# Values and gates in one product, and a new order of TensorE's work in the first pass of a macaron block

## The chip, the cores and the metric

One core of one Trainium2 chip. The time is the device time of one launch, in microseconds; the kernel before has a median of 1885.43 us over 3 runs (1883.06 to 1886.68).

## The reference, cut to what matters

The input x is 2 x 1024 tokens of 512 numbers. Three layers follow each other: half an FFN, an attention, and the same half FFN again.

```python
x = x + 0.5 * ffn(layernorm(x)); x = x + attn(layernorm(x)); x = x + 0.5 * ffn(layernorm(x))

def ffn(x):                       # 8 groups, 64 experts, 8 of them taken
    scores = softmax(x @ gate_w.T); top 8 -> w_e
    flat = w_e[:, inv_map]        # [token, group, 8]
    scalar = flat.sum(-1); soft = softmax(where(flat == 0, -1e9, flat))
    xg = x + soft @ mask_up_w     # per group
    a = silu(xg @ gate_proj.T) * (xg @ up_proj.T)
    return sum over groups of scalar * (a @ down_proj.T)

def attn(x):                      # gated linear attention, 4 heads, 64 values each
    q, k, v = x @ Wq, x @ Wk, x @ Wv
    gk = log_sigmoid(x @ Wgk1 @ Wgk2 + bgk2) / 16
    o = chunkwise recurrence over chunks of 64 tokens, with decay exp(gk)
    o = rms_norm(o) * Wnorm * silu(x @ Wg)
    return o @ Wo
```

All matrix products keep float32 accuracy: each operand is split into a high and a low part, and three products (high by high, high by low, low by high) are added in PSUM. `three` issues them.

## The kernel before, in words

The 2048 tokens are 4 blocks of 512. A **pass** (`p` or `q`, 0 to 7, called the first pass, pass 2 and so on in the text) is one FFN over one block; four of the passes (q = 1, 2, 4, 5) also carry the attention of a block. A pass has 22 **chunks** (`c`; `n` counts them over all passes) of 128 hidden rows of the FFN. For chunk n TensorE runs, in this order: `main` into bank GB (the gate sum, 12 matmuls of 512 columns), `soft` into the same bank (one matmul, line 1244: the routed part, whose weights are the product of mask_up_w and the chunk's weights), `main` into UB (the up sum, 12), `soft` into UB, and `down(n-1)` (12, into the four banks YB). Behind each of the three is a **slot**: `pieces(3n)`, `pieces(3n+1)`, `pieces(3n+2)` run the step k = 3c, 3c+1, 3c+2 of the attention of this pass and of the router of the next one. Step k does its part on each engine at that engine's place in its own program. Each engine works strictly in program order.

For chunk n ScalarE computes `sig` = Silu of GB, VectorE computes `act_t` = UB x sig x s_bc (`gate`), ScalarE rounds it into `a_hi` (`round_a`), VectorE subtracts into `a_lo` (`rest_a`), and `down` reads both.

In the first pass the weights are not yet split. Per chunk c SyncE's queue loads raw gate/up weights (`raw_gu`, a part of b_all) and down weights (`raw_d`, a part of k_all); ScalarE writes the high part (`gu_hi`, `d_hi`), VectorE the low part (`gu_lo`, `d_lo`), in `wt` or `tw`, and `dt`. Then TensorE multiplies mask_up_w by the chunk's weights (`masked`, 8 matmuls of 256 columns, lines 1229 and 1230), VectorE masks the result (`m_mask`, gt from bank and q_all), ScalarE and VectorE split it (`m_top`, `m_rest`, wt from gt), and `soft` reads it. GpSimd's queue stores the split weights to `scr_w` and `scr_d`, from where the later passes load them (`load_w`, `load_d`). Order in the first pass: TensorE ends chunk c with `masked(c+1)`; ScalarE has `gu_hi(c+1)` behind the Silu of chunk c; VectorE begins chunk c with `gu_lo(c+1)`, then `gate(c)`.

Router of the next pass, steps: 28 statistics, 31 norm, 32, 33, 35, 36 the four transposes with high and low parts of x (x_hi, x_lo), 38 logits, 39 to 50 the routing. Attention, steps: 7 to 11 transposes, 13 and 15 values, 14 the low-rank decay input, 16 to 19 the four decay logits, 20 and 21 gates, 22 to 29 queries and keys, from 30 on the recurrence. Its weights come in seven slabs per block, loaded by GpSimd's queue (`load_t`) and split at the steps that `SPLIT` names.

All engines are ordered by semaphores that only count up. TensorE's waits that matter here: `masked(c+1)` waits for `gu_lo(c+1)`; `soft` in the first pass waits for `m_rest` of its chunk (m_ok); the transposes of the router wait for the norm (xn_ok) and for the low part of the tile before.

Of the kernel before, what the change touches and what calls it, by code (L numbers as in the profile page):

```python
# [14 lines left out]
P = 128  # L15
# [26 lines left out]
S_V, S_G, S_QK, S_WO = 0, 1, 2, 6  # L42
# [20 lines left out]
def build(nc, x, wgu, wdn, wat, w_gate, w_mup, w_gk1, w_gk2, bgk, wnorm, inv, c_id, c_mask, c_reset, c_iota, out):  # L63
    with ExitStack() as ctx:
# [94 lines left out]
        def first_w(c):  # L159
# [34 lines left out]
        v_mm, g_mm, vt_ok, gt_ok, gtw_ok, z1_ok, zs_hi_ok, zs_ok, z_mm, zmin_ok, zabs_ok, zexp_ok, zln_ok = (  # L194
            sem(n) for n in ("v_mm", "g_mm", "vt_ok", "gt_ok", "gtw_ok", "z1_ok", "zs_hi_ok", "zs_ok", "z_mm", "zmin_ok",
# [44 lines left out]
        SPLIT = {4: S_V, 9: S_G, 16: S_QK, 22: S_QK + 1, 24: S_QK + 2, 26: S_QK + 3, 28: S_WO}  # L240
# [4 lines left out]
        def _(sp):  # L245
            def raw(c):
                j, half = c // 2, c % 2
                wait(sp, gu_lo_ok, c - 1)
                sp.dma_start(raw_gu[:, half, :], wgu[half, j]).then_inc(raw_gu_in[half], 16)
                wait(sp, d_lo_ok, c - 1)  # L250
                sp.dma_start(raw_d[:, half, :], wdn[half, j]).then_inc(raw_d_in[half], 16)
# [19 lines left out]
            raw(0)  # L271
            sp.dma_start(mask.rearrange("p a b -> p (a b)"), c_mask).then_inc(ld_mask, 16)
            raw(1)
            for c in range(2, CH):
                raw(c)
                if c == 2:
                    sp.dma_start(xr(1), x_t[1]).then_inc(ld_x[1], 16)
                if c == 4:
                    sp.dma_start(xr(2), x_t[2]).then_inc(ld_x[2], 16)
# [21 lines left out]
        def _(pool):  # L301
# [26 lines left out]
            def attention(t, q):  # L328
# [5 lines left out]
                load_t(t, S_V)  # L334
                rstd_of(LN_T[t])
                for n in range(S_G, S_QK + 2):
                    load_t(t, n)
                pool.wait_ge(gt_ok, 2 * t + 2)
# [44 lines left out]
            for q in range(1, PHASES):  # L383
                if FINAL[q - 1]:
                    store_out(q - 1)
# [8 lines left out]
        def _(act):  # L394
# [17 lines left out]
            def t_hi(t, s):  # L412
# [5 lines left out]
                elif s == S_QK + 1:  # L418
                    act.wait_ge(g_mm, 2 * t + 2)
                elif s == S_QK:  # L420
                    act.wait_ge(v_mm, 2 * t + 2)
# [4 lines left out]
                elif s == S_V:  # L426
# [63 lines left out]
            def attention(t, k, q):  # L490
                r, s = LN_T[t], (q + 1) % 2
                if k in SPLIT:
                    t_hi(t, SPLIT[k])
                if k in (7, 8, 10, 11):
# [4 lines left out]
                elif k == 14:  # L499
# [15 lines left out]
                elif k in (20, 21):  # L515
                    i = k - 20
                    act.wait_ge(g_mm, 2 * t + i + 1)
                    if i == 0:
                        wait(act, og_ok, t * H)
                    nc.scalar.activation(gt[:, 2 * i:2 * i + 2, :].rearrange("p a b -> p (a b)"), (W1, W0)[i][:],  # L520
                                         ACT.Silu).then_inc(gt_ok, 1)
# [111 lines left out]
            for p in range(PHASES):  # L633
                for c in range(CH):
# [6 lines left out]
                    round_a(n)  # L641
                    if n + 2 < PHASES * CH:
# [6 lines left out]
                    if p == 0 and 0 < c < CH - 1:  # L649
# [3 lines left out]
        def _(dve):  # L653
# [172 lines left out]
            def attention(t, k, q):  # L826
# [17 lines left out]
                elif k in (13, 15):  # L844
                    i = (k - 13) // 2
                    dve.wait_ge(v_mm, 2 * t + i + 1)
# [3 lines left out]
                    v = W0[:].rearrange("p (a v) -> p a v", v=DV)  # L850
                    z = vtz[:, 2 * i:2 * i + 2, :, :, :].rearrange("p t h r v -> p (t h) r v")
                    nc.vector.tensor_copy(z[0:CK, :, 0, :], v[0:CK, :, :])
                    nc.vector.tensor_copy(z[CK:P, :, 1, :], v[CK:P, :, :]).then_inc(vt_ok, 1)
                elif k == 14:
# [132 lines left out]
            for p in range(PHASES):  # L987
                for c in range(CH):
# [3 lines left out]
                    gate(n)  # L992
                    pieces(3 * n + 1)
                    rest_a(n)
                    if n == 1:
# [4 lines left out]
                    if p == 0 and 0 < c < CH - 1:  # L1000
# [6 lines left out]
        def _(pe):  # L1007
# [71 lines left out]
            def attention(t, k, q):  # L1079
                r, s = LN_T[t], (q + 1) % 2  # L1080

                def slab(n):
# [282 lines left out]
```

## Time and profile before

| | |
|---|---|
| median of 3 runs | 1885.43 us |
| profiled execution, its own time | 1883.3 us |
| span of its trace | 1881.6 us |
| TensorE busy | 1856.3 us (99%), 8896 matmuls |
| VectorE, ScalarE, GpSimd busy | 802.2, 528.2, 140.0 us |
| moved by DMA | 390.68 MB, mean 208 GB/s |
| mean granted TensorE clock | 0.997 |

A matmul's duration in the trace is that of the whole pipeline (390 ns for 512 columns), so neighbours overlap; how fast they follow each other is read from the difference of their starts. A line shows start and duration in us, engine, line, operation, output and inputs by name, partitions by elements, how many, and in brackets how long the engine was idle before it and what it waited for. PE is TensorE, ACT is ScalarE, DVE is VectorE, POOL is GpSimd, SP is SyncE; SPq is SyncE's DMA queue.

### The profile page before, as it was taken

The numbers are of one execution on the slowest core, as the hardware profiler recorded it, in microseconds if no ns is written. First come the engines' busy times: TensorE is split into PE (matmuls) and PEld (weight loads), VectorE is DVE, ScalarE is ACT, GpSimd is POOL, SyncE is SP. The second block draws the span as 40 slices with busy tenths as digits, with TensorE's granted clock in tenths as the row PEclk, the third lists the DMA queues.
The fourth block names the chain that finished last, engine by engine and source line by source line (L and its number), as shares of the span: only waits on it lengthen the run. The fifth ranks groups of instructions, "written<-read, shape, count | busy, mean of one in ns | idle before, by whom it ended". The sixth has DMA issues, their size and how long they took to land.

```text
span 1881.6 us, 22831 instructions
## 1 busy us (share of the span) xinstructions
PE 1856.3 (99%) x8896; PEld 1552.5 (83%) x8896; DVE 802.2 (43%) x1478; ACT 528.2 (28%) x802; POOL 140.0 (7%) x246
## 2 busy tenths in 40 slices
PE   6999999999999999999999999999999999999999
PEld 5887888888888888888888888888888888888887
DVE  6455553545354543323334455354544323322222
ACT  3333423433124432112212533123432111311111
POOL 1131110100000000000010000000000000000000
PEclk9999999999999999999999999999999999999999
DMA  6987875445564455576676454564455566567665
GB/s 198 318 279 247 276 283 199 154 156 179 191 232 151 159 172 193 193 248 210 210 254 222 164 193 163 188 231 168 156 173 179 200 239 214 210 214 261 220 235 175
DMA packets 94187, 390.68 MB, mean 208 GB/s; under 512 B 11936, under 2 KB 12320, under 8 KB 71552
## 3 DMA queue, kind: packets, MB, share of 16 engines
q1 hardware_dynamic: 54096, 286.74, 43.1%
q10 hardware_dynamic: 27600, 47.15, 9.6%
q0 software_dynamic: 12384, 55.32, 7.8%
q8 instruction: 72, 1.18, 0.3%
q14 instruction: 35, 0.29, 0.0%
HBM read 347.36 MB, written 41.81 MB: 207 GB/s over the span
## 4 chain that ended last, share of the span: by engine, by line
PE 94%; DVE 3%; DMA 1%; ACT 1%; issue 1%; SPq 0%; ACTq 0%; DVEq 0%
PE bank L1012 27%; PE bank L1014 27%; PE bank L1013 27%; PE bank L1244 4%; PE bank L1022 1%; PE bank L1185 1%; PE bank L1177 1%; PE bank L1184 1%; DMA b_all<-wgu 1%; PE bank L1171 1%; DVE act_t L655 0%; PE bank L1042 0%; PE bank L1229 0%; PE bank L1043 0%; PE bank L1230 0%
## 5 line engine op out<-in xcount | busy, mean ns | idle before, releaser
L1012 PE MATMUL bank<-x_hi,wt 128*128 128x512 f32 x1328 | 525.2, 395 | 0.2 <-issue 0.2
L1014 PE MATMUL bank<-x_lo,wt 128*128 128x512 f32 x1328 | 518.5, 390 | 0.0
L1013 PE MATMUL bank<-x_hi,wt 128*128 128x512 f32 x1328 | 518.2, 390 | 0.0
L655 DVE TENSOR_TENSOR act_t<-bank,sig 128x512 f32<-128x512 f32 x176 | 121.6, 691 | 557.9 <-PE bank L1244 556.3
L1014 PEld LDWEIGHTS bank<-x_lo,wt 128*128 128x128 f32 x1328 | 249.5, 188 | 53.0
L1012 PEld LDWEIGHTS bank<-x_hi,wt 128*128 128x128 f32 x1328 | 249.8, 188 | 49.9 <-issue 0.6
L1013 PEld LDWEIGHTS bank<-x_hi,wt 128*128 128x128 f32 x1328 | 249.9, 188 | 49.1
L1012 PE MATMUL bank<-dt,a_hi 128*128 128x512 f32 x704 | 279.7, 397 | 0.3 <-DVE a_lo L655 0.3
L1014 PE MATMUL bank<-dt,a_hi 128*128 128x512 f32 x704 | 275.4, 391 | 0.0
L1013 PE MATMUL bank<-dt,a_lo 128*128 128x512 f32 x704 | 274.6, 390 | 0.0
L581 ACT ACTIVATE sig<-bank 128x512 f32<-128x512 f32 x176 | 105.3, 598 | 479.4 <-PE bank L1244 479.4
L396 ACT ACTIVATE a_hi<-act_t 128x512 fp32r<-128x512 f32 x176 | 110.9, 630 | 372.5 <-DVE act_t L655 370.6
L655 DVE TENSOR_TENSOR a_lo<-act_t,a_hi 128x512 fp32r<-128x512 f32 x176 | 121.4, 690 | 157.9 <-ACT a_hi L396 157.3
L1014 PEld LDWEIGHTS bank<-dt,a_hi 128*128 128x128 f32 x704 | 132.2, 188 | 28.2
L1012 PEld LDWEIGHTS bank<-dt,a_hi 128*128 128x128 f32 x704 | 132.6, 188 | 26.5 <-issue 0.7
L1013 PEld LDWEIGHTS bank<-dt,a_lo 128*128 128x128 f32 x704 | 132.6, 188 | 25.9
L1244 PE MATMUL bank<-softT,wt 128*128 128x512 f32 x352 | 138.5, 395 | 9.6 <-DVE wt L655 9.3
L655 DVE TENSOR_TENSOR act_t<-s_bc,act_t 128x512 f32<-128x512 f32 x176 | 121.8, 692 | 6.3 <-DMA s_bc<-scr_s 0.3
L1244 PEld LDWEIGHTS bank<-softT,wt 128*128 128x128 f32 x352 | 66.2, 188 | 25.7 <-DVE wt L655 11.6
L1012 PE MATMUL bank<-x_hi,tw 128*128 128x512 f32 x208 | 82.2, 395 | 0.0
L1013 PE MATMUL bank<-x_hi,tw 128*128 128x512 f32 x208 | 82.1, 395 | 0.0
L1014 PE MATMUL bank<-x_lo,tw 128*128 128x512 f32 x208 | 82.0, 394 | 0.0
(178 smaller groups left out, 1748.5 us busy)
## 6 DMA issues: line engine op xcount, KB each, us to landing
wt<-scr_w SPq DMA_DIRECT2D x154, 1152.0 KB, 5.2
dt<-scr_d SPq DMA_DIRECT2D x154, 512.0 KB, 5.2
s_bc<-scr_s ACTq DMA_DIRECT2D x128, 256.0 KB, 5.3
state<-wat POOLq DMA_DIRECT2D x28, 512.0 KB, 5.3
scr_w<-wt POOLq DMA_DIRECT2D x12, 1024.0 KB, 5.1
b_all<-wgu SPq DMA_DIRECT2D x22, 512.0 KB, 7.4
scr_d<-dt POOLq DMA_DIRECT2D x22, 512.0 KB, 7.1
scr_w<-tw POOLq DMA_DIRECT2D x10, 1024.0 KB, 4.7
```

The costliest lines, as they stand in the source:

```text
L396: return nc.scalar.activation(dst, src, ACT.Copy)
L581: nc.scalar.activation(sig[:], g_bank(n)[:], ACT.Silu).then_inc(sig_ok, 1)
L655: return nc.vector.tensor_tensor(dst, a, b, op)
L1012: mm(dst, wh, xh, start=start, stop=False)
L1013: mm(dst, wl, xh, start=False, stop=False)
L1014: return mm(dst, wh, xl, start=False, stop=stop)
L1022: ins = nc.tensor.transpose(b[:, cols(k)], xn[:, i % 2, cols(k)], ident[:])
L1171: ins = mm(W0[:, cols(i)], b_all[:, h, cols(i)], q_all[:, h, cols(i)], start=True, stop=True)
L1177: ins = mm(W0[:, cols(i)], k2t[:, i, :], vtz[:, i, h, :, :], start=True, stop=True)
L1184: mm(W0[:, cols(i)], scm[:, h % 2, i, :], vtz[:, i, h, :, :], start=True, stop=False)
L1185: ins = mm(W0[:, cols(i)], q_all[:, h, cols(i)], state[:, h % 2, 2 * i:2 * i + 2, :], start=False, stop=True)
L1244: return mm(b[:], m[:, c0:c0 + P], softT[:, p % 2, c % 2, :], start=False, stop=True)
```

## The change

- The weights of values and gates are laid side by side: one product of 512 columns gives both for 128 tokens. It runs in steps 13 to 16, four groups of 12 matmuls into bank W0. VectorE copies the values out, then ScalarE takes Silu of the gates; the next group waits for that. Steps 20 and 21 fall away. Each of the two slabs holds two of the four parts of the inner dimension, so both are needed from step 13 on; the query/key slabs are split in steps 18 and 20 rather than 16 and 22.
- The first slab of an attention is loaded before the output stores of the pass before.
- First pass: SyncE issues gate/up load c+1 before down load c, and the inputs of blocks 1 and 2 behind chunks 4 and 7 rather than 2 and 4.
- First pass: `m_mask`, `m_top` and `m_rest` of chunk 2 stand in chunk 0's part of the program rather than in chunk 1's.
- First pass: TensorE runs both sums, with step 3n between them, and only then both soft matmuls. The other passes keep their order.

```diff
@@ -39,7 +39,7 @@
 SLABS = 7
-S_V, S_G, S_QK, S_WO = 0, 1, 2, 6
+S_VG, S_QK, S_WO = 0, 2, 6
@@ -237,16 +237,19 @@
-        SPLIT = {4: S_V, 9: S_G, 16: S_QK, 22: S_QK + 1, 24: S_QK + 2, 26: S_QK + 3, 28: S_WO}
+        SPLIT = {4: S_VG, 9: S_VG + 1, 18: S_QK, 20: S_QK + 1, 24: S_QK + 2, 26: S_QK + 3, 28: S_WO}
...
         def _(sp):
-            def raw(c):
+            def raw_gate_up(c):
                 j, half = c // 2, c % 2
...
                 sp.dma_start(raw_gu[:, half, :], wgu[half, j]).then_inc(raw_gu_in[half], 16)
+
+            def raw_down(c):
+                j, half = c // 2, c % 2
                 wait(sp, d_lo_ok, c - 1)
@@ -268,15 +271,20 @@
                 sp.dma_start(xr(0)[:, i, :], x_t[0][:, i, :]).then_inc(ld_x0[i], 16)
-            raw(0)
+            raw_gate_up(0)
+            raw_down(0)
             sp.dma_start(mask.rearrange("p a b -> p (a b)"), c_mask).then_inc(ld_mask, 16)
-            raw(1)
+            raw_gate_up(1)
+            raw_down(1)
+            raw_gate_up(2)
             for c in range(2, CH):
-                raw(c)
-                if c == 2:
-                    sp.dma_start(xr(1), x_t[1]).then_inc(ld_x[1], 16)
-                if c == 4:
-                    sp.dma_start(xr(2), x_t[2]).then_inc(ld_x[2], 16)
+
+                if c + 1 < CH:
+                    raw_gate_up(c + 1)
+                raw_down(c)
+                if c in (4, 7):
+                    b = (4, 7).index(c) + 1
+                    sp.dma_start(xr(b), x_t[b]).then_inc(ld_x[b], 16)
             for p in range(1, PHASES):
@@ -325,17 +333,19 @@
-            def attention(t, q):
+            def first_slab(t):
...
                     pool.wait_ge(o_ok, t * H)
-                load_t(t, S_V)
+                load_t(t, S_VG)
+
+            def attention(t, q):
                 rstd_of(LN_T[t])
-                for n in range(S_G, S_QK + 2):
+                for n in range(S_VG + 1, S_QK + 2):
                     load_t(t, n)
-                pool.wait_ge(gt_ok, 2 * t + 2)
+                pool.wait_ge(gt_ok, (t + 1) * NT)
                 if t == 0:
@@ -381,6 +391,8 @@
             for q in range(1, PHASES):
+                if q in ATT:
+                    first_slab(ATT[q])
                 if FINAL[q - 1]:
@@ -415,15 +427,13 @@
                     act.wait_ge(k_mm, t * H + s - S_QK - 1)
-                elif s == S_QK + 1:
-                    act.wait_ge(g_mm, 2 * t + 2)
-                elif s == S_QK:
-                    act.wait_ge(v_mm, 2 * t + 2)
+                elif s >= S_QK:
+                    act.wait_ge(vg_mm, (t + 1) * NT)
                 elif t == 0:
...
                     act.wait_ge(st_w[2 + s], 16 * len(range(2 + s, CH, 4)))
-                elif s == S_V:
+                elif s == S_VG:
                     act.wait_ge(k_mm, t * H)
@@ -491,12 +501,18 @@
                     t_hi(t, SPLIT[k])
+                if k in (13, 14, 15, 16):
+                    i = k - 13
+                    act.wait_ge(vt_ok, t * NT + i + 1)
+                    if i == 0:
+                        wait(act, og_ok, t * H)
+                    nc.scalar.activation(gt[:, i, :], W0[:, 2 * P:4 * P], ACT.Silu).then_inc(gt_ok, 1)
                 if k in (7, 8, 10, 11):
...
                     hi(r, i, s, (W0, W1)[i % 2])
-                elif k == 14:
+                if k == 14:
                     act.wait_ge(z1_ok, t + 1)
@@ -512,13 +528,6 @@
                         nc.scalar.activation(spl[:], spl[:], ACT.Ln, bias=1.0).then_inc(zln_ok, 1)
-                elif k in (20, 21):
-                    i = k - 20
-                    act.wait_ge(g_mm, 2 * t + i + 1)
-                    if i == 0:
-                        wait(act, og_ok, t * H)
-                    nc.scalar.activation(gt[:, 2 * i:2 * i + 2, :].rearrange("p a b -> p (a b)"), (W1, W0)[i][:],
-                                         ACT.Silu).then_inc(gt_ok, 1)
                 elif 22 <= k <= 29:
@@ -639,6 +648,8 @@
                     round_a(n)
+                    if n == 0:
+                        m_top(2)
                     if n + 2 < PHASES * CH:
@@ -646,7 +657,7 @@
                     pieces(3 * n + 2)
-                    if p == 0 and 0 < c < CH - 1:
+                    if p == 0 and 1 < c < CH - 1:
                         m_top(c + 1)
@@ -841,17 +852,16 @@
                         norm(r, i + 2, xb)
-                elif k in (13, 15):
-                    i = (k - 13) // 2
-                    dve.wait_ge(v_mm, 2 * t + i + 1)
+                if k in (13, 14, 15, 16):
+                    i = k - 13
+                    dve.wait_ge(vg_mm, t * NT + i + 1)
                     wait(dve, o_ok, t * H)
...
                         dve.wait_ge(zero_ok, 3)
-                    v = W0[:].rearrange("p (a v) -> p a v", v=DV)
-                    z = vtz[:, 2 * i:2 * i + 2, :, :, :].rearrange("p t h r v -> p (t h) r v")
-                    nc.vector.tensor_copy(z[0:CK, :, 0, :], v[0:CK, :, :])
-                    nc.vector.tensor_copy(z[CK:P, :, 1, :], v[CK:P, :, :]).then_inc(vt_ok, 1)
-                elif k == 14:
+                    v = W0[:, 0:2 * P].rearrange("p (h v) -> p h v", v=DV)
+                    nc.vector.tensor_copy(vtz[0:CK, i, :, 0, :], v[0:CK, :, :])
+                    nc.vector.tensor_copy(vtz[CK:P, i, :, 1, :], v[CK:P, :, :]).then_inc(vt_ok, 1)
+                if k == 14:
                     dve.wait_ge(zs_hi_ok, t + 1)
@@ -990,14 +1000,18 @@
                     gate(n)
+                    if n == 0:
+                        m_mask(2)
                     pieces(3 * n + 1)
                     rest_a(n)
+                    if n == 0:
+                        m_rest(2)
                     if n == 1:
...
                     pieces(3 * n + 2)
-                    if p == 0 and 0 < c < CH - 1:
+                    if p == 0 and 1 < c < CH - 1:
                         m_mask(c + 1)
@@ -1079,10 +1093,11 @@
-                def slab(n):
-                    n += t * SLABS
+                def slab(s):
+
+                    n = t * SLABS + s
                     pe.wait_ge(t_lo_ok, n + 1)
-                    w = tw[:, n % 2, :].rearrange("p (a k c) -> p a k c", a=2, k=KC)
+                    w = tw[:, n % 2, :].rearrange("p (a k c) -> p a k c", a=2, k=2 if s < S_QK else KC)
                     return w[:, 0, :, :], w[:, 1, :, :]
@@ -1099,20 +1114,18 @@
                     turn(r, i, (W0, W1)[i % 2])
-                elif k in (13, 15):
-                    n = (k - 13) // 2
-                    if n == 0:
+                if k in (13, 14, 15, 16):
+                    i = k - 13
+                    if i == 0:
                         pe.wait_ge(x_lo_ok, r * NT + 3)
...
                         pe.wait_ge(x_lo_ok, r * NT + 4)
-                        pe.wait_ge(vt_ok, 2 * t + 1)
-                    hi, lo = slab(S_V)
-                    for j in range(2):
-                        for kk in range(KC):
-                            ins = three(W0[:, cols(j, 2 * P)], xk(s, kk, cols(2 * n + j)), (hi[:, kk, :], lo[:, kk, :]),
-                                        kk == 0, kk == KC - 1)
-                    ins.then_inc(v_mm, 1)
-                elif k == 14:
+                        pe.wait_ge(gt_ok, t * NT + i)
+                    for kk in range(KC):
+                        hi, lo = slab(S_VG + kk // 2)
+                        ins = three(W0[:], xk(s, kk, cols(i)), (hi[:, kk % 2, :], lo[:, kk % 2, :]), kk == 0, kk == KC - 1)
+                    ins.then_inc(vg_mm, 1)
+                if k == 14:
                     pe.wait_ge(x_lo_ok, r * NT + 4)
@@ -1125,24 +1138,15 @@
                     elif h == 1:
-                        pe.wait_ge(vt_ok, 2 * t + 2)
+                        pe.wait_ge(gt_ok, (t + 1) * NT)
                     else:
...
                     mm((W1, W0)[h % 2][:], gk2_s[:, cols(h)], zs[:], start=True, stop=True).then_inc(z_mm, 1)
-                elif k in (20, 21):
-                    n = k - 20
-                    pe.wait_ge(zabs_ok, t * H + 3 + n)
-                    hi, lo = slab(S_G)
-                    for j in range(2):
-                        for kk in range(KC):
-                            ins = three((W1, W0)[n][:, cols(j, 2 * P)], xk(s, kk, cols(2 * n + j)), (hi[:, kk, :], lo[:, kk, :]),
-                                        kk == 0, kk == KC - 1)
-                    ins.then_inc(g_mm, 1)
                 elif 22 <= k <= 29:
...
                     if h == 0:
-                        pe.wait_ge(gt_ok, 2 * t + 1 + is_k)
+                        pe.wait_ge(zabs_ok, t * H + 3 + is_k)
                     else:
@@ -1172,7 +1176,7 @@
                         pe.wait_ge(sc_cp, t * H + h + 1)
-                        pe.wait_ge(vt_ok, 2 * t + 2)
+                        pe.wait_ge(vt_ok, (t + 1) * NT)
                         for i in range(NT):
@@ -1296,11 +1300,15 @@
                         main(GB, 0, p, c)
-                    soft(g_bank(n), 0, p, c).then_inc(g_ok, 1)
+                    if p:
+                        soft(g_bank(n), 0, p, c).then_inc(g_ok, 1)
                     pieces(3 * n)
...
                         main(UB, P, p, c)
+                    if p == 0:
+
+                        soft(g_bank(n), 0, p, c).then_inc(g_ok, 1)
                     soft(u_bank(n), P, p, c).then_inc(u_ok, 1)
```

## Rows read from the trace of the kernel before

**Rows 1.** Page, part 1: busy time of each engine, share of the span, instructions.

```profile
PE 1856.3 (99%) x8896; PEld 1552.5 (83%) x8896; DVE 802.2 (43%) x1478; ACT 528.2 (28%) x802; POOL 140.0 (7%) x246
```

**Rows 2.** Waits of TensorE: total us, times, longest.

```profile
PE bank L1022 <- DVE o_all L708: 10.3, 7, 6.5
PE bank L1244 <- DVE wt L655: 9.3, 5, 6.1
```

**Rows 3.** TensorE by stretch: stretch, length, busy (matmuls), granted clock, DMA.

```profile
40.30:46.40 6.10, 0.01 (x1) 0.66 0.91 257
46.40:52.50 6.10, 6.10 (x14) 0.50 0.96 375
```

**Rows 4.** Stretch behind the first pass: PE, PEld, DVE, ACT, POOL, clock, DMA.

```profile
254.00:1881.00 1627.00, 1622.13 (x7782) 1358.91 (x7780) 664.46 (x1220) 437.29 (x658) 93.60 (x157) 1.00 0.58 199
```

**Rows 5.** Timeline of TensorE, pass 2, first group of values and what follows.

```profile
295.61 0.28 PE L1012 MATMUL bank<-tw,x_hi 128*128 128x256 f32 x1
295.72 0.28 PE L1013 MATMUL bank<-tw,x_lo 128*128 128x256 f32 x1
...
298.48 0.40 PE L1012 MATMUL bank<-dt,a_hi 128*128 128x512 f32 x1
298.71 0.40 PE L1013 MATMUL bank<-dt,a_lo 128*128 128x512 f32 x1
```

**Rows 6.** Timeline of VectorE, a copy of 256 columns out of PSUM.

```profile
28.09 0.42 DVE L756 COPY tb<-bank 128x256 f32<-128x256 f32 x1 [0.61 <-PE bank L1059]
```

**Rows 7.** Timeline, pass 2, last decay logit and the chunk's a_lo.

```profile
321.37 0.39 PE L1131 MATMUL bank<-zs,gk_s 128*128 128x512 f32 x1
...
331.50 0.69 DVE L655 TENSOR_TENSOR a_lo<-act_t,a_hi 128x512 fp32r<-128x512 f32 x1 [7.85 <-ACT a_hi L396]
```

**Rows 8.** Timeline of the start: TensorE, VectorE, ScalarE, SyncE's queue.

```profile
37.41 0.40 PE L1012 MATMUL bank<-x_hi,tw 128*128 128x512 f32 x1
...
41.37 0.51 SPq L249 DMA_DIRECT2D b_all<-wgu  x1
...
45.02 0.42 DVE L655 TENSOR_TENSOR gt<-bank,q_all 128x256 f32<-128x256 f32 x1
...
46.38 0.80 PE L1244 MATMUL bank<-softT,wt 128*128 128x512 f32 x1 [6.09 <-DVE wt L655]
...
54.33 1.06 ACT L396 ACTIVATE tw<-b_all 128x1024 fp32r<-128x1024 f32 x1 [6.52 <-DMA b_all<-wgu]
...
65.84 0.39 PE L1244 MATMUL bank<-softT,wt 128*128 128x512 f32 x1
```

**Rows 9.** Timeline, chunk 7 of the first pass: soft, gu_lo, masked.

```profile
101.38 0.39 PE L1244 MATMUL bank<-softT,wt 128*128 128x512 f32 x1
...
103.38 1.23 DVE L655 TENSOR_TENSOR wt<-b_all,wt 128x1024 fp32r<-128x1024 f32 x1 [3.22 <-ACT wt L396]
...
107.27 0.29 PE L1229 MATMUL bank<-wt,og 128*128 128x256 f32 x1
```

**Rows 10.** Timeline, chunks 10 and 11: soft, norm (x2), soft, gu_lo.

```profile
131.23 0.50 PE L1244 MATMUL bank<-softT,wt 128*128 128x512 f32 x1 [0.71 <-DVE wt L655]
...
136.07 1.00 DVE L708 TENSOR_SCALAR o_all<-x_res,mv,rstd 128x512 f32<-128x512 f32 x2
...
141.39 0.40 PE L1244 MATMUL bank<-softT,wt 128*128 128x512 f32 x1
...
144.95 1.22 DVE L655 TENSOR_TENSOR wt<-b_all,wt 128x1024 fp32r<-128x1024 f32 x1
```

**Rows 11.** Timeline, end of the first pass: soft, mask store, first load, first matmul.

```profile
237.29 0.39 PE L1244 MATMUL bank<-softT,wt 128*128 128x512 f32 x1
...
241.34 0.54 POOL L316 DMA_DIRECT2D scr_w<-wt  x1
...
247.65 3.00 SPq L260 DMA_DIRECT2D wt<-scr_w  x2
...
253.18 0.47 PE L1012 MATMUL bank<-x_hi,wt 128*128 128x512 f32 x1 [0.22 <-issue]
```

**Rows 12.** Timeline of TensorE, chunk 14 of the first pass.

```profile
175.99 0.50 PE L1244 MATMUL bank<-softT,wt 128*128 128x512 f32 x1 [1.38 <-DVE wt L655]
```

More of the change, by code:

```diff
@@ L193, in build @@
         dve_step = sem("dve_step")
-        v_mm, g_mm, vt_ok, gt_ok, gtw_ok, z1_ok, zs_hi_ok, zs_ok, z_mm, zmin_ok, zabs_ok, zexp_ok, zln_ok = (
-            sem(n) for n in ("v_mm", "g_mm", "vt_ok", "gt_ok", "gtw_ok", "z1_ok", "zs_hi_ok", "zs_ok", "z_mm", "zmin_ok",
+        vg_mm, vt_ok, gt_ok, gtw_ok, z1_ok, zs_hi_ok, zs_ok, z_mm, zmin_ok, zabs_ok, zexp_ok, zln_ok = (
+            sem(n) for n in ("vg_mm", "vt_ok", "gt_ok", "gtw_ok", "z1_ok", "zs_hi_ok", "zs_ok", "z_mm", "zmin_ok",
                              "zabs_ok", "zexp_ok", "zln_ok"))
@@ L1335 @@
     heads = [np.concatenate([fold(f[n][:, h * P:(h + 1) * P]) for n in ("attn_Wq", "attn_Wk")], axis=-1) for h in range(H)]
-    wat = np.stack([w.reshape(P, GW) for w in (fold(f["attn_Wv"]), fold(f["attn_Wg"]), *heads, fold(f["attn_Wo"]))])
+    values_gates = np.concatenate([fold(f["attn_Wv"]), fold(f["attn_Wg"])], axis=-1)
+    wat = np.stack([w.reshape(P, GW) for w in (values_gates[:, 0:2], values_gates[:, 2:4], *heads, fold(f["attn_Wo"]))])
     inv = f["ffn_inv_map"]
```

## Prediction

> **What bounds the kernel now.** I read the page's first part, then the waits of TensorE, the granted clock by stretch, and the timeline of the first pass. TensorE is busy in 1856.3 of 1881.6 us, VectorE in 43%, ScalarE in 28% [rows 1]. So only two things can shorten the run: fewer TensorE cycles, or less TensorE waiting. Its waits [rows 2] come to about 22 us: 10.3 before transposes, 6.5 of them for the first input, and 9.3 before the routed (soft) matmuls, L1244, one of them 6.1 us. A stretch view shows a second price of that one: in the 6.1 us after it the clock is 0.50, which is 1.2 GHz [rows 3]. From 254 us to the end TensorE is busy in 1622 of 1627 us [rows 4]: there is nothing to win there but cycles. Spacings below are differences of starts: 120 ns for 256 columns (24 matmuls from 295.61 to 298.48), 227 ns for 512 (26 from 101.38 to 107.27) [rows 5, 9].
>
> **Part 1: values and gates joined.** Before, each attention block runs 96 matmuls of 256 columns, in four groups of 24; after, 48 of 512, in four groups of 12. One group of 24 takes 298.48 - 295.61 = 2.87 us [rows 5]; twelve of 512 take 12 x 0.227 = 2.72. That is 0.15 x 4 groups x 4 blocks = **-2.4 us**. Bounds: -3 and 0; it is nothing if the joined ones come at 0.239.
> At this place the Trainium skill can be weighed (page "TensorE: Matmul & The Clock Gate", section "Back-to-back issue gap"): a warm matmul takes N / 2.4 + 2.5 ns. By it 24 take 2.62 us and 12 wide ones 2.59, so the join would give 0.5 us over all blocks. The rows are slower than the rule at both widths, and more so at 256.
>
> Does a wait take its place? The four groups share one bank: group i+1 waits for ScalarE's gate of group i, which waits for VectorE's two value copies, and ScalarE's a_hi and VectorE's a_lo of the chunk are queued behind them. Nearest row: 0.42 us for 256 columns out of PSUM [rows 6]. So 0.2 drain + 0.43 + 0.43 + 0.45 = 1.5 us, under the 12 matmuls (2.72 us) between two groups. Hidden with 1.2 us to spare; without that cover each of 12 gaps would pay the difference. a_lo is late by 3 us and needed 10 later.
> The gates' 5.8 us also leave the place between the fourth decay logit and the first query, where ScalarE does Abs, Exp and Ln and only then a_hi. There the last logit matmul starts at 321.37 and a_lo is ready at 332.19: 10.8 us [rows 7]; a slab's splitting, now queued in front, adds 0.3. The down product that needs it now comes after 51 matmuls, 11.6 us. Hidden by 0.5 us. Taken: 0, bounds 0 and +4 us. The first slab's load goes ahead of four output stores on GpSimd's queue, once; no TensorE wait hangs on either: 0.
>
> **Part 2: start of the first pass.** The 6.1 us wait is for VectorE's m_rest of chunk 2, whose m_mask ran at 45.02 [rows 8]. It stands in the program behind gate(1), a_lo, the decay weights and d_lo. TensorE had done its masked product by 37.4. The change issues m_mask after gate(0), at 38.3; m_top follows a_hi(0) on ScalarE, m_rest ends at 40.2. That delays d_lo(0) and what is behind it by some 0.9 us. Meanwhile TensorE has 24 matmuls ahead of the soft pair, from 37.41 to 42.86. So this wait goes, and the low clock with it. Next late would be gate/up load 3: issued at 41.37, because SyncE's queue stood behind a down load that waits for d_lo(0), and used at 54.33 as it landed [rows 8]. The change issues it at about 17.8, when gu_lo(1) is done. The two input loads of 1 MB go later, to chunks 4 and 7; the first is needed in chunk 9. From 42.86: soft pair 0.45, down(0), down(1) 5.45, masked 0.97, gate and up sums 5.45, soft of chunk 3 at 55.2, its second at 55.4. Before, that second one started at 65.84. **-10.4 us**.
>
> **Part 3: the steady first pass, where the new order costs.** T is the start of a chunk's gate soft matmul. It releases Silu, then gu_hi, then gu_lo, which ends at T + 3.23 [rows 9]. The next chunk's masked product (L1229) needs gu_lo, and the sums wait behind it. Before, 26 matmuls lay between, and it came at T + 5.9 [rows 9]. Now 14 do: T + 3.18. It waits until 3.29, and a first pair after a wait is some 0.09 slower: 0.19 us. In chunks 3 to 8 this is +0.9 (0.2 of waiting there is in the old time), in 17 to 20 +0.8: **+1.7 us**. In chunks 9 and 13 to 15 VectorE's chain bounds as before and starts 0.2 us sooner: **-0.6 us**.
> In chunk 10 the first router transpose stands behind down. It needs VectorE's norm, behind gate(10), done at 136.6 = T + 5.4 [rows 10]. Before, TensorE came at T + 5.9. Now it comes at T + 3.2 and waits until T + 5.2: +2.0. In chunk 11 gu_lo ends at 146.17 = T + 4.78, because x_lo before it waits for ScalarE [rows 10]; the masked product, one transpose (0.44) later than T + 3.2, waits 1.1. Another transpose that needs x_lo loses 0.3. With the slower first pairs: **+3.7 us**.
>
> **Part 4: the end of the first pass.** The first weight load of pass 2 is issued at 247.65, when the store of mask part 20 has landed; that store was issued at 241.34 behind the 1 MB store that follows gu_lo(21). TensorE starts on it at 253.18, 0.4 us late [rows 11]. From the soft matmul of chunk 20 (237.29) that chain is 15.89 us. TensorE will need 3.29 + 0.09 + 0.97 + 5.45 + 0.45 + 2.72 = 13.0 us from there, not 15.5. The wait becomes 2.9: **+2.5 us**. The chain itself isn't changed.
>
> **Sum.** -10.4 + 1.7 - 0.6 + 3.7 + 2.5 = -3.1 in the first pass, -2.4 in the joined products: -5.5 us. Two new holes, of 2.0 and 2.9 us, may cost clock. After the hole of 6.1 us 13 matmuls ran at 0.427 instead of 0.227, 2.6 us [rows 3]; a hole of 1.4 us cost none [rows 12]. Bounds 0 and 5.2; I take 1.3, half of one, since the 2.9 lies between them. Result -4.2: profiled execution 1883.3 - 4.2 = 1879.1 us (its span is 1.7 less). The median shown, 1885.43, lies 2.1 above that execution: **1881.2 us**.
>
> **Rivals.**
> A: the late costs don't come (parts 3 and 4 near 0): -10.4 - 2.4 = -12.8, 1872.6 us; with half of them 1876. For it: VectorE is idle over half the time. Against: the order of gu_lo, norm and the last stores stays, and their times are rows. 0.25.
> B, slower: the cover behind the decay logits. It decides from 0.5 us of slack. If ScalarE's Abs, Exp, Ln chain comes 2.5 us later than reckoned, TensorE stands 2 us before down in each of four blocks: +8, the sum +3.8, 1889 us. For it: it is the thinnest cover of the passes with attention, and slab splitting is queued before it. Against: 0.3 of shift is all that I find. 0.1.
> C: both new holes bring the low clock in full: -5.5 + 5.2 = -0.3, 1885.1, no change. For it: 2.0 and 2.9 are longer than any later hole of the trace. 0.2.
> D: the join gives nothing, the wide matmuls coming at 0.239: -5.5 + 2.4 + 1.3 = -1.8, 1883.6. Against: 512 columns out of tw run at 0.227 elsewhere. 0.05. The Trainium skill's rule of part 1 would give 1883.1; the rows contradict it.
> My own sum: 0.4.
>
> **Chances.** 0.2% is 3.8 us, about what a measurement of this kernel can tell from none. Faster (under 1881.7): A's 0.25 and somewhat more than half of mine, with a remainder, 0.54. Within: 0.34. Slower: B and a little, 0.12. Range 1875.0 to 1886.0: beyond half of A at the low end, C at the high one.
>
> **What would show it.** Right: no wait near 40 us and full clock there; the soft pair of chunk 3 at 55; masked products waiting 0.1 us each for VectorE's wt or tw; a transpose wait of 2 us in chunk 10; a wait of 2.5 to 3 us at the first load of pass 2; joined matmuls 0.227 apart and no wait before down in the attention passes. Wrong: a wait still at chunk 2's soft matmuls, down products waiting for a_lo in passes 2, 3, 5 and 6, or a long stretch at 1.2 GHz after a short hole.

## The result, and the profile after

The changed kernel takes **1887.84 us** (median of 22 runs, 1885.17 to 1890.78), the kernel before, on the same chip, 1885.13 (22 runs, 1882.40 to 1888.55). The ratio is 1.0015, 95% interval 1.0009 to 1.0021: 2.7 us slower, within the 3.8 us called no change, and 6.6 us above the forecast of 1881.2. The profiled execution took 1887.89 us, its span 1886.2.

The first part of the page of the changed kernel, the answer to [rows 1]:

```profile
PE 1857.4 (98%) x8704; PEld 1540.2 (82%) x8704; DVE 810.2 (43%) x1494; ACT 529.6 (28%) x810; POOL 140.6 (7%) x246
```

There are 192 matmuls fewer (48 x 4 blocks), and yet TensorE is busy 1.1 us longer. Its waits, the answer to [rows 2] (total us, times, longest):

```profile
PE bank L1036 <- DVE o_all L719: 12.1, 7, 6.5
PE bank L1026 <- DVE a_lo L666: 5.0, 5, 1.2
PE bank L1026 <- issue: 3.4, 1, 3.4
PE bank L1248 <- DVE wt L666: 1.9, 3, 1.0
PE bank L1056 <- DVE x_lo L666: 1.5, 1, 1.5
PE bank L1233 <- DVE wt L666: 0.9, 1, 0.9
```

The 6.1 us before a soft matmul are gone. In their place stand 5.0 us before `down` for a_lo, which was 0.3 before, 3.4 us at one load, and 1.8 us more before a transpose.

Where the time came and went is read best from the start of the same matmul in both traces (the later of the two soft matmuls of chunk n, which both kernels run in the same place). After minus before, us:

| chunk | 3 | 9 | 10 | 11 | 12 | 17 | 21 | 22 | 30 | 52 | 110 | 175 |
|---|---|---|---|---|---|---|---|---|---|---|---|---|
| before at | 65.84 | 123.70 | 134.31 | 144.83 | 155.35 | 211.42 | 249.85 | 258.97 | 352.61 | 611.88 | 1234.23 | 1871.81 |
| after - before | -9.81 | -8.86 | -9.12 | -7.00 | -5.44 | -5.07 | -4.30 | +1.73 | +2.46 | +3.19 | +3.87 | +4.59 |

So 9.8 us are won by chunk 3. Of these 5.5 are lost over the rest of the first pass, 6.0 more at its end, between chunks 21 and 22, and 0.72 in each of the four attention blocks.

**The start** (timeline of the changed kernel; the answer to [rows 8]):

```profile
39.04 0.42 DVE L666 TENSOR_TENSOR gt<-bank,q_all 128x256 f32<-128x256 f32 x1
...
43.25 0.62 PE L1248 MATMUL bank<-softT,wt 128*128 128x512 f32 x2
...
45.48 1.05 ACT L408 ACTIVATE tw<-b_all 128x1024 fp32r<-128x1024 f32 x1
46.56 1.23 DVE L666 TENSOR_TENSOR tw<-b_all,tw 128x1024 fp32r<-128x1024 f32 x1
```

The mask product runs at 39.04 instead of 45.02. The two soft matmuls follow behind both sums with no wait in front of them, and the high part of gate/up chunk 3 is written at 45.48, where it stood at 54.33 waiting for its load.

**Chunks 10 and 11** (timeline; the answer to [rows 10]; the bracket is the idle time before the instruction and what ended it):

```profile
125.19 0.40 PE L1248 MATMUL bank<-softT,wt 128*128 128x512 f32 x1
...
129.44 1.21 DVE L719 TENSOR_SCALAR o_all<-x_res,mv,rstd 128x512 f32<-128x512 f32 x2
...
130.23 0.63 PE L1036 MATMUL bank<-ident,o_all 128*128 128x128 f32 x4 [1.91 <-DVE o_all L719]
...
141.16 1.22 DVE L666 TENSOR_TENSOR wt<-b_all,wt 128x1024 fp32r<-128x1024 f32 x1
...
142.43 0.39 PE L1233 MATMUL bank<-wt,og 128*128 128x256 f32 x1 [0.93 <-DVE wt L666]
```

The transpose comes at the end of `down`, 3.2 us behind the soft matmuls, and stands until VectorE's norm is there.

**The end of the first pass** (timeline; the answer to [rows 11]):

```profile
235.53 0.61 PE L1248 MATMUL bank<-softT,wt 128*128 128x512 f32 x2
...
239.58 0.55 POOL L324 DMA_DIRECT2D scr_w<-wt  x1
...
245.11 2.38 SPq L263 DMA_DIRECT2D wt<-scr_w  x2
...
252.11 0.77 PE L1026 MATMUL bank<-x_hi,wt 128*128 128x512 f32 x1 [3.45 <-issue]
```

Behind it, by stretch (stretch, length, PE, PEld, DVE, ACT, POOL, granted clock, DMA share, GB/s):

```profile
252.20:258.00 5.80, 5.80 (x14) 4.54 (x15) 0.00 (x0) 0.00 (x0) 0.00 (x0) 0.50 1.00 361
```

TensorE stood 3.45 us, and then ran at 0.50, which is 1.2 GHz, until 257.8: 13 matmuls at 0.427 instead of 0.227, 2.6 us. The kernel before paid the same 2.6 us behind its 6.1 us wait [rows 3], so nothing is saved there. Experiment 4, where neither stretch exists, is busy for 1854.2 us. Where the rest of the 1.1 us comes from stays open.

**An attention block** (timeline, pass 2; last decay logit, then what a_lo waits for; the answer to [rows 7]):

```profile
319.80 0.39 ACT L509 ACTIVATE gt<-bank 128x256 f32<-128x256 f32 x1 [5.29 <-DVE vtz L863]
...
326.72 1.23 DVE L666 TENSOR_TENSOR tw<-state,tw 128x1024 fp32r<-128x1024 f32 x1 [3.42 <-ACT tw L408]
...
328.18 0.39 PE L1144 MATMUL bank<-zs,gk_s 128*128 128x512 f32 x1
328.25 0.53 POOL L334 DMA_DIRECT2D state<-wat  x1 [39.61 <-DVE tw L666]
...
328.79 2.41 POOL L351 TENSOR_TENSOR gt<-gt,wn 128x1024 f32<-128x1024 f32 x1
329.24 2.51 DVE L666 TENSOR_TENSOR act_t<-s_bc,act_t 128x512 f32<-128x512 f32 x1
...
331.68 0.74 DVE L874 TENSOR_SCALAR tb<-bank,bias 128x512 f32<-128x512 f32 x1
332.51 0.69 ACT L525 ACTIVATE b_all<-bank,bias 128x512 f32<-128x512 f32 x1 [3.12 <-DVE tb L874]
333.22 1.28 ACT L528 ACT_TABLE_LOAD   x1
334.51 1.92 ACT L528 ACTIVATE b_all<-b_all 128x2048 f32<-128x2048 f32 x1
...
340.28 0.69 DVE L666 TENSOR_TENSOR a_lo<-act_t,a_hi 128x512 fp32r<-128x512 f32 x1 [7.86 <-ACT a_hi L408]
341.11 0.47 PE L1026 MATMUL bank<-dt,a_hi 128*128 128x512 f32 x1 [1.16 <-DVE a_lo L666]
```

VectorE's product `act_t<-s_bc,act_t` takes 2.51 us. The same instruction takes 0.69 elsewhere: of the 176 in the launch only the four that meet GpSimd's multiply by Wnorm, one per block, are long. GpSimd's multiply had begun 0.45 us earlier and ended at 331.20. Behind the product wait, one after the other, the last decay logit's copy, Abs, Exp, Ln, a_hi, a_lo and `down`. In the kernel before, the same multiply ran from 334.37 to 336.77, since it waited for the second group of gates (timeline of the kernel before):

```profile
334.37 2.40 POOL L341 TENSOR_TENSOR gt<-gt,wn 128x1024 f32<-128x1024 f32 x1 [18.90 <-ACT gt L520]
```

No product of VectorE with two inputs in SBUF started beside it there. The join makes the last gate ready before the decay logits, at 320.2, and so the gates no longer hold the multiply back. What then sets its moment stands ahead of it in GpSimd's program: the load of the next query/key slab, which waits until VectorE has split the slab before it. That split now stands in step 18 rather than 16. It ends at 327.95, the load is issued at 328.25, and the multiply follows at 328.79, right before the product. In the kernel before this load was issued at 314.94, long before the gates. The order is the same in all four blocks.

### The profile page after: what moved, and what is told of

Read it like the earlier page. It is cut to its first block, busy times and chain, and to the rows that moved or that the text cites. A ratio compares the mean times of both kernels' runs of the same rounds, so it can differ in the third digit from the quotient of the medians.

```text
span 1886.2 us, 22478 instructions
## 1 busy us (share of the span) xinstructions
PE 1857.4 (98%) x8704; PEld 1540.2 (82%) x8704; DVE 810.2 (43%) x1494; ACT 529.6 (28%) x810; POOL 140.6 (7%) x246
## 4 chain that ended last, share of the span: by engine, by line
PE 91%; DVE 4%; ACT 3%; issue 2%; DMA 0%; POOL 0%; ACTq 0%; SPq 0%; DVEq 0%; POOLq 0%
PE bank L1026 26%; PE bank L1028 26%; PE bank L1027 26%; PE bank L1248 4%; PE bank L1036 1%; DVE act_t L666 1%; PE bank L1189 1%; PE bank L1181 1%; PE bank L1188 1%; PE bank L1233 1%; PE bank L1175 1%; PE bank L1234 0%; PE bank L1056 0%; PE bank L1057 0%; ACT b_all L528 0%
## 5 line engine op out<-in xcount | busy, mean ns | idle before, releaser
L1248 PE MATMUL bank<-softT,wt 128*128 128x512 f32 x352 | 134.5, 393 | 2.2 <-DVE wt L666 1.9
L666 DVE TENSOR_TENSOR act_t<-s_bc,act_t 128x512 f32<-128x512 f32 x176 | 129.1, 734 | 6.7 <-DMA s_bc<-scr_s 0.7
```

Source lines behind the costliest of these rows:

```text
L666: return nc.vector.tensor_tensor(dst, a, b, op)
L1248: return mm(b[:], m[:, c0:c0 + P], softT[:, p % 2, c % 2, :], start=False, stop=True)
```

## The experiments

Ten kernels were run, in three groups, each group beside runs of the kernel before on one chip (medians there 1884.86, 1883.97 and 1884.30). A trace's table means the comparison above, against the trace of before.

**1. Without GpSimd's multiply.** This kernel leaves the factor Wnorm out of the attention's output.

```diff
-                pool.wait_ge(gt_ok, (t + 1) * NT)
-                nc.gpsimd.tensor_tensor(gt[...], gt[...], wn[...], ALU.mult).then_inc(gtw_ok, 1)
...
-                dve.wait_ge(gtw_ok, t + 1)
+                dve.wait_ge(gt_ok, (t + 1) * NT)
```

> The changed kernel without GpSimd's multiply of the gates by Wnorm (left out, so the output lacks that factor). Theory L (the port): VectorE's second gate product stood 2.5 us instead of 0.69 because GpSimd's multiply ran at the same time, and that alone makes a_lo late for the down product; then that product takes 0.69 again in all four attention passes, the four waits of 1.2 us before down are gone, and the time is 5.3 us under the changed kernel's 1887.8, so 1882.5. Theory G (the queue: moved gates' Silu and the slab splitting in front of the decay logits make the chain late by themselves): the four waits stay at 1 us or more, and the time is within 1 us of 1887.8.

Measured: 1881.40 us, ratio 0.9979 (0.9970 to 0.9988), 6.8 us under the changed kernel by the ratios. The waits for a_lo are gone, all but the 0.3 us of before, and all 176 products take 0.69. So the multiply is what delays the chain.

**2. The multiply later.** It is issued behind the router's statistics on GpSimd (with the last slab loads ahead of it), where VectorE's gate products are not beside it. Nothing is left out.

```diff
-                [multiply of gt by wn, in attention(t, q)]
+            def norm_weight(t): [the same multiply]
...
                 if q in ATT:
+                    norm_weight(ATT[q])
                     attention_tail(ATT[q])
```

> The changed kernel with the same multiply, but put behind the router's rstd on GpSimd, where VectorE is idle in the trace (about 380 to 385 us in pass 2). Theory L: as without the multiply, 1882.5, no wait before down. A weaker form of it, in which any GpSimd work lengthens the chain, would leave part of the waits or put new ones at the transposes of 390 us (0.7 us each). Theory G: no change, 1887.8.

Measured: 1881.24 us, 0.9980 (0.9972 to 0.9989). The multiply runs at 374.59 in pass 2, with no instruction of VectorE beside it. The place of the old collision in its trace (timeline):

```profile
325.86 0.69 DVE L669 TENSOR_TENSOR act_t<-s_bc,act_t 128x512 f32<-128x512 f32 x1
...
329.31 1.92 ACT L531 ACTIVATE b_all<-b_all 128x2048 f32<-128x2048 f32 x1
...
335.07 0.69 DVE L669 TENSOR_TENSOR a_lo<-act_t,a_hi 128x512 fp32r<-128x512 f32 x1 [7.86 <-ACT a_hi L411]
```

The last decay logit starts at 324.79 in this trace and a_lo ends at 335.76: 10.97 us, the 10.8 of [rows 7] and almost nothing more. In the changed kernel it was 340.97 - 328.18 = 12.79; the difference, 1.82, is that of the product (2.51 - 0.69). Each block now gives -0.72 in the table.

**3. The gate's soft matmul ahead of the up sum again**, in the first pass; all else as changed.

```diff
-                    if p:
-                        soft(g_bank(n), 0, p, c).then_inc(g_ok, 1)
+                    soft(g_bank(n), 0, p, c).then_inc(g_ok, 1)
                     pieces(3 * n)
...
-                    if p == 0:
-                        soft(g_bank(n), 0, p, c).then_inc(g_ok, 1)
```

> The changed kernel with the gate's soft matmul back ahead of the up sum in the first pass; all else as changed. Theory S (the new order costs all through the first pass what the early mask of chunk 2 wins): no wait at the masked products, none of 2 us in chunk 10, the hole at the end of the pass back from 3.6 to about 0.4 us and no low clock behind it. Pass 2 then starts some 9 us under before at chunk 3 and still 9 to 10 under it at the end of the pass; time 1887.8 - 11.5 = 1876.3. A small wait of 0.1 to 0.3 us at chunk 2's soft matmul. Rival R (the order is needed for the start): chunk 2 waits 2 us or more and the gain is under 7 us.

Measured: 1877.43 us, 0.9961 (0.9948 to 0.9975), 10.2 us under the changed kernel by the ratios. In the table it stays at -9.6 from chunk 9 to 13 and at -8.97 at chunk 22, where the changed kernel has +1.73. The holes of chunks 10 and 11 and of the end are gone and the clock is 1.000. The mask's product, now needed sooner, costs one wait, in chunk 2 (timeline of TensorE):

```profile
40.68 0.50 PE L1248 MATMUL bank<-softT,wt 128*128 128x512 f32 x1 [0.38 <-DVE wt L666]
```

**4. The mask's store ahead of the 1 MB store**, at chunk 20 of the changed kernel, on GpSimd's queue: the first load of pass 2 waits for that store.

```diff
+                if c == CH - 2:
+                    store_m(c)
                 if c + 1 < CH:
                     store_w(c + 1)
-                store_m(c)
+                if c != CH - 2:
+                    store_m(c)
```

> The changed kernel with one pair of GpSimd's stores swapped in chunk 20: the mask part goes ahead of the 1 MB of weights. Theory E (the first load of pass 2 waits for the mask store behind the 1 MB store): the hole of 3.6 us at about 248 shrinks to under 1.5 us, and the 13 matmuls at the low clock behind it run at full clock: 2 to 3.6 us plus 2.7 us, so 1881.5 to 1883.2. Rival: the load waits for the weight stores themselves, or the load's own 5 us are the end of the chain; hole within 0.5 us of before, time 1887.8.

Measured: 1883.17 us, 0.9992 (0.9983 to 1.0000), 4.3 us under the changed kernel by the ratios. The hole at the first load is gone, and the next load comes late (waits of TensorE):

```profile
PE bank L1029 <- DMA wt<-scr_w: 1.8, 1, 1.8
```

No low clock follows. So the hole at the first load is a matter of the stores' order, as reckoned, and part of it returns one load later: 2.1 us between chunks 22 and 23 in the table.

**5. Experiments 2 and 3 together.**

> The changed kernel with both: the gate's soft matmul back ahead of the up sum, and the multiply by Wnorm late on GpSimd. If the two costs are separate they add: 1885 - 9.0 (start, measured in the run with the old soft order) - 2.4 (join) = 1873.6, no wait before down, no low clock. If the late multiply meets other VectorE work once the first pass is shorter: 1875 to 1877 with new waits at the transposes of the attention passes.

Measured: 1871.89 us, 0.9934 (0.9920 to 0.9947), 12.4 us faster than before and 1.7 under the forecast sum. The two costs are separate: no wait for a_lo is left but the 0.3 us of before, and the clock is 1.00. Its longest waits of TensorE, and its stretch behind the first pass:

```profile
PE bank L1039 <- DVE o_all L722: 10.0, 7, 6.6
PE bank L1251 <- DVE wt L669: 3.7, 5, 1.4
PE bank L1059 <- DVE x_lo L669: 1.5, 1, 1.5
```

```profile
254.00:1869.00 1615.00, 1611.75 (x7557) 1341.68 (x7556) 665.81 (x1234) 438.47 (x665) 92.79 (x155) 1.00 0.58 198
```

**6. The join and the early first slab alone**: the first pass's order, its loads and its mask as before.

> The join and the first slab alone, on the kernel before (first pass as before). Sum of my reading: -2.4 for the joined products, +5.3 for four waits before down behind GpSimd's multiply: +2.9, 1887.9, with the 6.1 us wait and its low clock as in the kernel before. If the wait before down came only because the passes start at another phase of the transfers, it is gone here: 1882.6.

Measured: 1886.01 us, 1.0012 (1.0003 to 1.0020): the join by itself, with its collision, makes the kernel some 2 us slower. The waits for a_lo are there with the first pass untouched, and so is the old one before soft (waits of TensorE):

```profile
PE bank L1234 <- DVE wt L656: 10.3, 6, 6.5
...
PE bank L1012 <- DVE a_lo L656: 5.0, 5, 1.2
```

In its table each of the four blocks adds 0.70 to 0.72, as in the changed kernel.

**7. The early mask alone**, on the kernel before.

```diff
                     gate(n)
+                    if n == 0:
+                        m_mask(2)
...
-                    if p == 0 and 0 < c < CH - 1:
+                    if p == 0 and 1 < c < CH - 1:
                         m_mask(c + 1)
```

(`m_top` and `m_rest` likewise.)

> The early m_mask, m_top and m_rest of chunk 2 alone, on the kernel before (old order of loads, of soft matmuls, old values and gates). Theory N (the next wait takes its place): gate/up load 3 is still issued at about 41.5 and lands near 54, so the masked product of chunk 3 waits for gu_lo(3) from 49 to 56.6, some 7.5 us, with low clock behind it: the gain is at most 1.2 us, time 1884 to 1885.5. Theory M (the mask alone is the fault): the 6.1 us and the clock are won, 8.7 us, 1876.3.

Measured: 1885.42 us, 1.0004 (0.9995 to 1.0013), no gain (timeline):

```profile
43.32 0.39 PE L1250 MATMUL bank<-softT,wt 128*128 128x512 f32 x1
...
54.25 1.06 ACT L396 ACTIVATE tw<-b_all 128x1024 fp32r<-128x1024 f32 x1 [9.52 <-DMA b_all<-wgu]
55.34 1.23 DVE L657 TENSOR_TENSOR tw<-b_all,tw 128x1024 fp32r<-128x1024 f32 x1 [9.73 <-ACT tw L396]
56.62 0.58 PE L1235 MATMUL bank<-tw,og 128*128 128x256 f32 x1 [7.48 <-DVE tw L657]
```

The wait of 6.1 us before chunk 2's soft matmul has become one of 7.5 us before chunk 3's masked product, because the load of gate/up 3 still lands at 54.

**8. The new order of the loads alone**, on the kernel before (the hunk of SyncE's queue in the diff).

> The kernel before with the new order of the input loads alone; chunk 2's mask stays late. Theory N (the mask's place and the load's place each hide the other's wait, so that only both together give the 10 us; the early mask alone gave nothing): the wait before chunk 2's soft matmul stays, since VectorE's mask product still runs behind gate(1), and gate/up load 3 is no longer late but nobody waited for it. No change, -1 to +0.5 us. Theory M (the loads were the larger half all along, and the early mask is not needed): -8 to -10 us, and no wait near 46 us.

Measured: 1884.15 us, 0.9997 (0.9987 to 1.0007), no gain either: the load is there in time (the high part of gate/up 3 is written at 47.88), and the old wait stays (timeline of TensorE):

```profile
46.55 0.79 PE L1252 MATMUL bank<-softT,wt 128*128 128x512 f32 x1 [6.22 <-DVE wt L663]
```

**9. Both, on the kernel before**, without the join and with the old order of the soft matmuls.

> The early mask of chunk 2 and the new order of SyncE's loads together, on the kernel before, without the new order of the soft matmuls and without the join. Theory N: together they win what neither does alone: soft matmul of chunk 3 some 9.5 us earlier, and 9 us at the end of the pass, 1876.0; chunk 2 waits 0.5 us or less. If the order of the soft matmuls were needed too, chunk 2 would wait over 2 us and the gain would be under 7.

Measured: 1874.75 us, 0.9954 (0.9941 to 0.9967): 8.7 us faster. Two edits that are each worth nothing are worth nearly 9 together.

**10. Experiment 5 with both soft matmuls behind the sums in chunk 2 alone.**

```diff
+                    if n != 2:
                         soft(g_bank(n), 0, p, c).then_inc(g_ok, 1)
                     pieces(3 * n)
...
+                    if n == 2:
+                        soft(g_bank(n), 0, p, c).then_inc(g_ok, 1)
```

> The best version so far (old order of the gate's soft matmuls, GpSimd's multiply late) with the new order of the soft matmuls kept in chunk 2 alone, where the profile of the old order has a wait of 0.5 us for the mask. If the new order helps wherever VectorE's split weights come after the gate sum and hurts only where it shortens the cover of the next chunk: the 0.5 us go, chunk 3's masked product has two matmuls fewer of cover and may wait 0.2 of them; 0 to -0.5 us against that version, so 1871.5. If the order costs in any chunk: +0.2 or more against it, 1872.1 or above. The difference is near what the spans can show; the start of the soft matmul of chunk 3 tells it.

Measured: 1872.06 us, 0.9930 (0.9916 to 0.9945). That can't be told from experiment 5's 0.9934. In the traces the wait before chunk 2's soft matmul is gone, and from chunk 1's second soft matmul to chunk 3's TensorE takes 19.55 us, where experiment 5 takes 20.04. But the same stretch takes 19.89 in experiment 3 and 19.49 in experiment 9, both with the old order: the wait for the mask differs from trace to trace, from 0.55 us to nothing. So whether the new order in chunk 2 is worth 0.5 us or nothing stays open.

## Why the prediction was wrong

Worked out in the prediction's own terms, on the profiled executions, in us (the table of chunks above is called the table):

| term | forecast | measured | read from |
|---|---|---|---|
| start of first pass | -10.4 | -9.8 | table, chunk 3 |
| steady first pass, chunks 3 to 21 | +1.7 - 0.6 + 3.7 = +4.8 | +5.5 | -4.30 + 9.81 |
| end, the hole | +2.5 | +3.2 | from the last matmul's start to the first that uses the load: 3.84, before 0.61 |
| low clock | +1.3 | +2.8 | the rest of 1.73 + 4.30; 13 matmuls x 0.20 are 2.6 of it |
| join, cycles | -2.4 | -2.9 | 4 x (-0.72), experiment 2 |
| join, cover behind the decay logits | 0 | +5.8 | 4 x (0.72 + 0.72), changed kernel and experiment 2 |
| sum (of unrounded terms) | -4.2 | +4.6 | |

**The step that failed** is in part 1: "Hidden by 0.5 us. Taken: 0". The arithmetic of that step was right as far as it went: without the collision the chain takes 10.97 us (experiment 2) where 10.8 and 0.3 were reckoned, and TensorE's 11.6 us cover it. What was left out is where the change moves GpSimd's multiply. It waits for the last gate (`gt_ok` stands in the diff) and stands behind a slab's load. The gates come some 14 us earlier, the load waits for the split that the change puts in step 18, and so the multiply falls on VectorE's product. The chain grows by 1.82 us and eats the 0.5. What is left is 1.32 us of waiting per block, and the first matmuls behind the wait follow each other more slowly, 0.1 more. Experiments 1, 2 and 6 each show that from another side. That the split's step decides the moment is read from the traces; no run has the multiply in its old place in the program and the split elsewhere. Rival B named the right place, the right releaser and the point from which it decides (0.5 us of slack); it had neither this cause nor this size (8 us against 5.8) and was given 0.1. The step's upper bound of 4 us was too low as well.

The row and a rule agree here. VectorE's product was held from 329.24, GpSimd's multiply ended at 331.20, and the product ended 0.55 later. The product just before it, `act_t<-bank,sig`, has one input in PSUM; it also overlapped the multiply and took 0.68, as elsewhere. The Trainium skill, page "SBUF — State Buffer", sections "Who interferes with whom" and "SBUF: two separate sides", states that a VectorE instruction with two SBUF inputs and a GpSimd instruction that reads SBUF exclude each other through a shared port, and that whichever starts second is blocked for the whole of the other. By that rule the question for the join was not only how long the gates take but what VectorE does when the multiply starts.

**The second miss** is the price of a hole: two terms mis-sized, by 0.7 and 1.5 us. The chain behind the hole of 2.9 us was said not to change. From chunk 20's first soft matmul it was 15.89 us and became 252.11 - 235.53 = 16.58. The store of the mask landed sooner (9.58 us from soft to the issue of the load, 10.36 before), but from its issue to TensorE's first matmul the load took 7.00 us, not 5.53. In experiments 1 and 2, whose first pass is the same program, it took 7.28 and 5.92, so its length also differs from trace to trace. DMA engines were busy 0.96 of the time from 247.5 to 252.5, and 0.87 from 248 to 253 before; that this traffic is the cause is argued, not shown. And the low clock came in full, where half was taken. Experiment 2, with a hole of 2.2 us in this place, had none.

**Right.** Part 2: the wait near 40 is gone, the clock there is 1.00, and the second soft matmul of chunk 3 starts at 56.03 (forecast 55.4). Experiments 7 to 9 show its two halves, mask and load, to be needed together, as its text has them one behind the other: "Next late would be gate/up load 3". Part 3: the masked products lose 0.1 to 0.2 each (-9.81 to -8.86 over six chunks, forecast +0.9), chunks 10 and 11 cost 3.7 (-9.12 to -5.44, forecast 3.7), with the forecast waits of 2.0 and 1.1 us showing 1.91 and 0.93, and chunks 17 to 21 0.8 (forecast 0.8). Only the -0.6 of chunks 9 and 13 to 15 (by its own 0.2 for each of four chunks it should have been -0.8) came out as +0.1: chunks 9 and 13 gave 0.3 each, chunk 12 lost 0.15 and chunk 14 0.5. The loss of chunk 14 stands in the tables of all kernels with the new order of the loads (+0.6 between chunks 14 and 15 in experiments 3, 5, 8, 9 and 10) and not in that of experiment 7, so it belongs to the loads. Part 4's mechanism: experiment 4 removes the hole. The join's cycles: with the collision gone, each block gives -0.72 (experiment 2), against -0.6. The joined matmuls follow each other at 0.227, as read from the trace of the changed kernel (timeline of TensorE, pass 2):

```profile
302.78 0.39 PE L1026 MATMUL bank<-tw,x_hi 128*128 128x512 f32 x1
303.01 0.39 PE L1027 MATMUL bank<-tw,x_lo 128*128 128x512 f32 x1
...
305.27 0.40 PE L1028 MATMUL bank<-tw,x_hi 128*128 128x512 f32 x1
```

Twelve from 302.78 at 0.227 are 2.72 us, and no wait stands between the groups. So rival D falls, and with it the 0.5 us that part 1 worked out by a rule of the Trainium skill: measured are 2.9 us, and the 2.4 from the rows was nearer. The section that part 1 names gives its formula for an isolated matmul, and here it is 0.01 us short at both widths (0.120 and 0.227 measured).

**The parts priced by medians** (differences of ratios x 1885). The start gives 8.7 us (experiment 9). The join with its collision costs 2.3 (experiment 6), of which the collision is 5.1 (experiment 3 to 5, 0.9961 to 0.9934), so the join without it is worth about 2.8. Experiments 1 and 2 put the collision higher, at 6.8 and 6.6; the 5.8 of the traces lies between. The order of the soft matmuls in the first pass costs 10.2 (experiment 3), where the prediction's terms for it, 4.8 + 2.5 + 1.3, make 8.6. It is the largest single cost of the change, and its sign and most of its size were in the forecast; the collision, which was not, is what took the sum from faster to slower.

## What to carry to other kernels

When an edit makes a value ready earlier, follow everything that waits for that value, on idle engines too, to its new place. That place may be set by what stands ahead of it in its own queue. Ask what it lands beside: here a multiply that nobody waited for stretched a product on another engine from 0.69 to 2.51 us. A wait that stands on two late inputs is worth nothing until both are early (0 and 0 alone, 8.7 us together), so before an edit to the head of a chain is dropped, look for what is late next. And work that is moved out from between two dependent steps (12 matmuls between soft and masked) gives no cycle back; it only takes the cover away, here for 10 us.

## What the runs showed of the hardware that was not expected

TensorE's clock after a hole is not a function of the hole's length alone. In chunk 10 the changed kernel stood 1.91 us before the transpose and ran on at 1.00, while experiment 1 stood 1.90 us in the same place and fell to 1.2 GHz for some 3.4 us (a granted clock of 0.59 over 4.2 us is 0.50 for 82% of it). The same stretch in both, first the changed kernel, then experiment 1:

```profile
129.30:133.50 4.20, 3.27 (x21) 2.97 (x22) 3.94 (x8) 1.98 (x4) 1.64 (x3) 1.00 0.98 375
```

```profile
129.30:133.50 4.20, 4.20 (x19) 3.73 (x18) 3.24 (x7) 1.32 (x3) 0.53 (x1) 0.59 1.00 379
```

Experiment 2 stood 1.88 us and fell too (0.61 in this stretch); experiment 4 stood 1.89 and did not. All four run the same program up to there, so in four traces it went either way twice. What decides stays open. None of the kernels without a hole of this length behind the wait for the first input (experiments 3, 5, 9 and 10) shows a mean clock under 1.000 in its trace. For a forecast this means that a new hole of about 2 us carries a chance of some clock besides its own length: chunk 10 cost 2.1 us in the two traces that kept the clock, and 3.7 in the two that did not.
